# One-hot tables laid out in groups of four, and the rank phase of a graph kernel written out, on one core

## The reference

```python
edge_index = jnp.stack([src, dst])                       # dst is sorted, src is not
# layer 0: B = exp(-edge_weight); out = segment_sum(B[:, None] * x[dst], src); x = layernorm(x + out)
# layer 1: segment_sum, segment_max and mean of edge_attr_32 by src; an MLP of them; x = layernorm(x + h)
# layer 2: two graph convolutions, segment_sum by dst with degree norms; x = layernorm(x + out)
# layer 3: attention over the edges of each dst, softmax, segment_sum by dst; x = layernorm(x + y)
```

## Time and profile before

| | us |
|---|---|
| median of 3 runs (10755.75 to 10773.13) | 10757.1 |
| the profiled execution's own time | 10722.97 |
| its span | 10721.2 |
| busy: PE 27%, DVE 48%, ACT 7%, POOL 65% of the span | |
| granted clock of TensorE, mean (as a share of 2.4 GHz) | 0.547 |

### The profile page before, as it was taken

How to read it: one execution, slowest core, us unless ns; L and a number is a source line. 1 busy time by engine, 2 the same in 40 slices (tenths; PEclk the granted TensorE clock), 3 DMA queues, 4 the chain that set the end, 5 groups by cost and what they waited for, 6 DMA issues and landing times.

```text
span 10721.2 us, 73942 instructions
## 1 busy us (share of the span) xinstructions
PE 2920.0 (27%) x14214; PEld 2646.6 (25%) x14214; DVE 5184.4 (48%) x18978; ACT 768.3 (7%) x2419; POOL 6928.5 (65%) x6880
## 2 busy tenths in 40 slices
PE   9999888888600130000000200000002000000000
PEld 9998777777500130000000200000002000000000
DVE  5558777777699632222222222222224455555555
ACT  0003222222200010000000000000000000000000
POOL 0407777777700427777777577777777777777775
PEclk9995555555555565555555555555555555555555
DMA  5002222222277402222222122222221222222221
GB/s 226 12 7 77 72 72 75 72 72 75 75 272 273 144 24 54 52 52 54 52 52 54 37 53 53 52 54 52 52 54 27 60 58 61 58 61 59 59 60 37
DMA packets 541044, 766.54 MB, mean 71 GB/s; under 512 B 328408, under 2 KB 341632, under 8 KB 527600
## 3 DMA queue, kind: packets, MB, share of 16 engines
q1 hardware_dynamic: 321008, 509.44, 14.1%
q0 software_dynamic: 219904, 255.88, 11.1%
HBM read 352.03 MB, written 412.82 MB: 71 GB/s over the span
## 4 chain that ended last, share of the span: by engine, by line
POOL 62%; issue 21%; PE 9%; DVE 7%; DMA 1%; POOLq 0%; ACT 0%; DVEq 0%; SPq 0%; ACTq 0%
POOL arena_a L573 43%; POOL by_src L522 15%; PE bank L693 7%; POOL arena_a L542 3%; DVE arena_a L1096 2%; DVE arena_a L1091 2%; POOL adst_at_start L556 1%; PE bank L787 1%; PE bank L809 1%; DVE arena_b L1175 0%; DVE stat L1172 0%; DVE stat L1176 0%; DVE x L1174 0%; DVE x L1182 0%; DVE cap_blk L1053 0%
## 5 line engine op out<-in xcount | busy, mean ns | idle before, releaser
L573 POOL DMA_INDIRECT arena_a<-table_c,decay x3136 | 2968.3, 947 | 1190.5 <-issue 955.0
L1282 DVE SCALAR_TENSOR_TENSOR arena_a<-arena_a,same_dst 128x64 f32<-128x64 f32 x3134 | 893.4, 285 | 3000.3 <-DMA arena_a<-table_c,decay 2894.9
L522 POOL DMA_INDIRECT by_src<-arena_b,idx_blk x1568 | 1627.1, 1038 | 756.3 <-issue 497.4
L573 POOL DMA_INDIRECT arena_a<-table_at,decay x1568 | 1637.0, 1044 | 477.9 <-issue 477.9
L767 PE MATMUL bank<-ident,chunk_end 128*64 128x128 f32 (+2 forms) x8 | 2.7, 442 | 6147.6 <-DVEq L842 6147.6
L767 PEld LDWEIGHTS bank<-ident,chunk_end 128*64 128x64 f32 (+2 forms) x8 | 1.4, 240 | 6148.2 <-DVEq L842 6148.2
L735 PE MATMUL bank<-arena_b 98*128 98x128 f32 x3136 | 988.2, 418 | 226.0 <-DVE arena_b L992 226.0
L735 PEld LDWEIGHTS bank<-arena_b 98*128 98x128 f32 x3136 | 815.8, 310 | 277.6 <-DVE arena_b L992 277.6
L728 PE MATMUL bank<-arena_b 128*98 128x128 bf16 x1568 | 801.3, 511 | 1.6 <-ACT arena_b L654 1.0
L693 PE MATMUL bank<-arena_b 128*98 128x128 bf16 x3136 | 737.6, 415 | 16.5 <-DVE arena_b L921 16.5
L693 PEld LDWEIGHTS bank<-arena_b 128*98 128x98 bf16 x3136 | 736.8, 259 | 17.0 <-DVE arena_b L921 17.0
(11 more groups left out here) (260 smaller groups left out, 5317.7 us busy)
## 6 DMA issues: line engine op xcount, KB each, us to landing
states_src<-arena_a SPq DMA_DIRECT2D x98, 1024.0 KB, 4.8
states_c<-arena_a SPq DMA_DIRECT2D x196, 512.0 KB, 2.7
hrows<-by_src SPq DMA_DIRECT2D x98, 776.0 KB, 6.1
states_at<-arena_a SPq DMA_DIRECT2D x98, 576.0 KB, 3.3
x_at_start<-arena_a SPq DMA_DIRECT2D x7, 7168.0 KB, 48.4
arena_b<-x_at_start SPq DMA_DIRECT2D x98, 512.0 KB
arena_a<-table_c,decay POOLq DMA_INDIRECT x3136, 2.4
arena_b<-in_a SPq DMA_DIRECT2D x98, 256.0 KB, 3.5
```

The source lines that it names most:

```text
L522: pool.indirect_dma_start(out=by_src, out_offset=AT(ap=idx_blk[h][:, k:k + 1], axis=0), in_=rows[h][:, k, :], in_offset=None)\
L573: pool.indirect_dma_start(out=gb[r][:, k * w:(k + 1) * w], out_offset=None, in_=table[g], in_offset=AT(ap=src_i[:, n * J + k:n * J + k + 1 ...
L1282: ins = v.scalar_tensor_tensor(out=st[h][:, k * D:(k + 1) * D], in0=old, scalar=same_dst[:, e:e + 1], in1=gb[r][:, k * D:(k + 1) * D], op0 ...
```

## The change

- **Layout.** The one-hot tables become `[group][node digit][4 tiles]`. A matmul now reads every 4th value: its operands step by 8 bytes in place of 32. The tables of numbers are 4 wide and are repeated over the groups by the access pattern. This holds for both histograms and for the rank phase.
- **The rank phase is written out** on SP, POOL, ACT, PE and DVE, with constants for all waits. The histograms stay loops.
- **No copies.** Digits, masks and source numbers are read in place from `digits`, `same_dst` and `src_f`.
- **Four buffers** of `rows` and `idx_blk`, with `scattered0` to `scattered3`. To make room, `xs` and `xb` move from `arena_b` to `arena_a`.
- SP issues the attributes of a block one block earlier than before, right behind that block's features.

```diff
-        iota_hi = early["ih"].bitcast(bf16).rearrange("p (n t) -> p n t", t=J)
-        iota_lo = early["il"].bitcast(bf16).rearrange("p (n t) -> p n t", t=J)
+        iota_hi = early["ih"].bitcast(bf16).rearrange("p (n t) -> p n t", t=Q)
+        iota_lo = early["il"].bitcast(bf16).rearrange("p (n t) -> p n t", t=Q)
+        def in_groups(table):
+            return table.rearrange("p (g n) t -> p g n t", g=1).to_broadcast([P, J // Q, table.shape[1], Q])
+        def spread(digit, n):
+            return digit.rearrange("p (g o t) -> p g o t", o=1, t=Q).to_broadcast([P, J // Q, n, Q])
+        def one(onehot, k):
+            return onehot[:, k // Q, :, k % Q]
...
+            for n in range(-1, NBLK):
+                if n + 1 < NBLK:
+                    if n >= 1:
+                        sp.wait_ge(s("rows_ready"), n)
+                    m, h = n + 1, (n + 1) % 2
+                    sp.dma_start(early[f"xs{h}"], rows_of(x_at_start, D)[:, m * (J * D):(m + 1) * (J * D)])\
+                      .then_inc(s(f"xs_in{h}"), 16)
+                    if m >= R:
+                        sp.wait_ge(*scattered(m))
+                    sp.dma_start(rows[m % R][:, :, D:D + E32], a32_v[:, m * J:(m + 1) * J, :])\
+                      .then_inc(s(f"a32_in{m % R}"), 16)
...
-                        v.tensor_tensor(oh_hi[h], iota_hi, bf(digits[o, "hi"][:, at], HIGH), ALU.is_equal)
-                        v.tensor_tensor(oh_lo[h], iota_lo, bf(digits[o, "lo"][:, at], LOW), ALU.is_equal)\
+                        v.tensor_tensor(oh_hi[h], in_groups(iota_hi), spread(digits[o, "hi"][:, at], HIGH), ALU.is_equal)
+                        v.tensor_tensor(oh_lo[h], in_groups(iota_lo), spread(digits[o, "lo"][:, at], LOW), ALU.is_equal)\
                             .then_inc(s("onehots"), 1)
...
-                            last = pe.matmul(hist, oh_hi[h][:, :, k], oh_lo[h][:, :, k], start=False, stop=False)
+                            last = pe.matmul(hist, one(oh_hi[h], k), one(oh_lo[h], k), start=False, stop=False)
...
+            for n in range(NBLK):
+                v.wait_ge(s(f"xs_in{n % 2}"), (n // 2 + 1) * 16)
+                for quad in range(J // Q):
+                    g = n * (J // Q) + quad
+                    stage_a(g)
+                    if g:
+                        stage_b(g - 1)
+                    if quad == 1 and n + 1 < NBLK:
+                        v.wait_ge(s("hist_added"), n * J + 1)
+                        onehots_of(n + 1)
+            stage_b(L // Q - 1)
```

More of the change, by code:

```diff
@@ L320, in rows_of, with scattered @@
             return dram_ap.rearrange("(p l) w -> p (l w)", p=P)
[L322 to L324 removed]
+        def scattered(n):
+            return s(f"scattered{n % R}"), n // R * (16 * J)
         def blk(i, h):
@@ L752, in _ @@
-            pe.wait_ge(s("tile_onehots"), 1)
-            for k in range(Q):
-                turn(0, k)
-            turns(pe, body)
+            pe.wait_ge(s("tile_onehots"), 1)
+            for t in range(Q):
+                turn(t)
+            for t in range(L):
+                h, k, g = t // J % 2, t % J, t // Q
+                pe.wait_ge(s("snap_ready"), t + 1)
+                pe.matmul(hist, one(oh_hi[h], k), one(oh_lo[h], k), start=False, stop=True,
+                          skip_group_check=True).then_inc(s("hist_added"), 1)
+                if t % Q == 0:
+                    pe.wait_ge(s("hi_t_ready"), g + 1)
+                    if g >= 2:
+                        pe.wait_ge(s("selected"), (g - 1) * Q)
+                at = slice(t % Q * P, (t % Q + 1) * P)
+                last = pe.matmul(p_cnt[g % 2][:, at], hi_t[g % 2][:, at], snap[t % 2], start=True, stop=True)
+                if t % Q == Q - 1:
+                    last.then_inc(s("counted"), 1)
+                ahead = (g + 1) * Q
+                if t % Q < 2 and ahead < L:
+                    if t % Q == 0:
+                        if ahead % J == 0:
+                            pe.wait_ge(s("tile_onehots"), ahead // J + 1)
+                        if g:
+                            pe.wait_ge(s("ranked"), g)
+                    turn(ahead + t % Q * 2)
+                    turn(ahead + t % Q * 2 + 1)
@@ new lines, in stage_a @@
+            def stage_a(g):
+                for t in range(g * Q, (g + 1) * Q):
+                    n, k = t // J, t % J
+                    h = n % 2
+                    old = xb[h][:, k - 1, :] if k else xb[1 - h][:, J - 1, :] if n else first_row[:, :]
+                    if t:
+                        v.wait_ge(s("v_tiles"), t)
+                    v.scalar_tensor_tensor(out=xb[h][:, k, :], in0=old, scalar=same_dst[:, t:t + 1],
+                                           in1=xs[h][:, k, :], op0=ALU.mult, op1=ALU.add).then_inc(s("v_tiles"), 1)
+                    if t % Q == 0:
+                        v.wait_ge(s("src_spread"), g + 1)
+                    rank = v.scalar_tensor_tensor(out=junk[t % 2], in0=p_src[g % 2][:, t % Q * P:(t % Q + 1) * P],
+                                                  scalar=src_f[:, t:t + 1], in1=before[:, :],
```

218 lines of the change are left out of this document (63 added, 155 removed).

## The result

| us | before | after |
|---|---|---|
| median | 10757.61 (10755.75 to 10773.13, 4 runs) | 10349.16 (10336.82 to 10352.99, 4 runs) |
| ratio | | 0.9615, 95% interval 0.9599 to 0.9632 |
| the profiled execution's own time | 10722.97 | 10336.82 |
| its span | 10721.2 | 10335.0 |

A forecast was written before the change was run, and what follows sets the result against it. PE was taken to bound the histograms and POOL's scatters the rank phase; later passes' gathers stay untouched. Terms -310 - 4 + 0 = -314 took the median from 10757 to 10443 us, range 10370 to 10550.

The forecast's parts named there:

- the rank phase: Scatter phase limited by POOL: removed work worth nothing there, shifted meetings with DVE's instructions taken as 0, bounds -50 and +60.
- The histograms: Both histograms: smaller operand step cuts a block from 3.76 to 2.18 us, saving 310 us.
- the round's other part: Histograms' round through two buffers: 2.64 us besides PE's 16 tiles, for two blocks.
- the half clock: Histogram matmuls: 0.107 us a tile at a step of 8 bytes, taking PE at 1.2 GHz.
- The rival of a partial gain: Histograms: each new line still costs, 0.13 to 0.2 us a tile; at 0.17 saves 214, 10543 us; 14%.
- no gain: Histograms: the step doesn't matter at 8 bytes, histograms as before, 10753 us; 7%.
- slower one-hots: Grouped one-hots fall to one value a cycle on DVE: histograms +27, rank phase +162, 10942 us; 9%.
- The node scatter: POOL's 98 scatters beside the second histogram: about one a block, 214 us, ending with it; costed at nothing, no margin.
- Ahead of the first scatter: Before the rank phase's first scatter: fewer copies and less DVE waiting for PE, -4 us.
- My sign of error for this phase: Rank phase: scatters with a mean off 1038 ns by over 40 would show the prediction wrong.
- POOL's gaps at 0.30: Rank phase: POOL limited by its own 1568 x (0.959 + 0.30) us, with no waits to remove.
- The profiled execution and the median: Whole kernel: the median taken 34 us above the profiled execution, so 10409 became 10443 us.

The follow-up runs named there:

- doubled kernels: POOL scatters each tile twice, the second time into a tensor nothing reads, in the changed kernel (12311.0 us), it with features early (12348.0) and the kernel before (12667.4).
- e7_act_rows: The changed kernel with the multiplication of a block's rows by decay moved from DVE to ACT: 12152.8 us against 11792.7 for the changed kernel, with stalls.

## What the prediction had right, and where it failed

The direction and the main term were right; the time, 10349, lies 21 us below the range. The step that failed is the rank phase, put at 0 with bounds of -50 and +60: its scatters took 69.6 us less.

- **The histograms: right.** -305.3 against -310. The price of a tile was not 0.107 but 0.118, and the round's other part 2.53 us in place of 2.64 (DVE restarts earlier), so the two errors nearly cancelled: 2.21 us a block against 2.18. The reason given for 0.107, the half clock, was wrong: the granted clock was 0.78, and at 1.00 a tile takes 0.118 as well. Lines set it. With the price of a line read off 0.235/128 = 1.84 ns and 64 lines at a step of 8, the rows of before would have given 0.118, though no row of before shows that the price goes by lines. The rival of a partial gain is true in its mechanism, each new line costs, but at the price of 0.118 and not 0.17. The two rivals of no gain and of slower one-hots are false: 0.97 and 1.22 us as before.
- **The node scatter: the answer right, the mechanism too dear.** I had one scatter a block and no margin. It is 1.77 us from one to the next and 46 us of margin, since 38 of the 98 scatters aren't held up at all.
- **Ahead of the first scatter**: -5.4 against -4.
- **The rank phase: this step failed.** "At a random phase L1003 would cost about half its length, 0.6, and the pair of one-hots as much, 1.2 in all. I take 0." The multiplication did cost 0.61 where it met a scatter, 0.5 a block. (Before, it met one in 78 of 98 blocks, so it was 0.75 a block and not the 0.96 that I had.) The one-hots did not cost as much: 0.18 a block, all other meetings together 28 us, so the excess fell by 50 us, to the very bound of -50. What I had wrong is that the one-hots fall at random. They follow the multiplication at a fixed distance, and a scatter that it holds up restarts POOL at a fixed time after it (it ends 0.83 us after, the next ones follow 1.26 apart); so wherever the multiplication itself stands, the one-hots stand at the same place of a scatter. In the three kernels without stalls that have the new layout and no copies they cost 18.0, 18.4 and 18.7 us; in the kernel before, at a distance 1.00 us longer, 43.6, and doubled 27.8. With stalls POOL starts from another point, and the same one-hots cost 80. This is read from the timelines; no run changes the distance alone. That the multiplication's part is the phase, and that the phase comes from the order of two issues on SP, is shown by the doubled kernels, where it is worth 34 us; for the change itself, at 16 scatters a block, it is inferred from the same drop, 0.94 to 0.61. My sign of error for this phase, a mean off 1038 ns by over 40, was too wide: it was off by 32, which is 50 us.
- **The pauses were missed.** The longest "issue" of POOL was 2.1 us in the earlier trace rows, where all others are 0.3. I priced POOL's gaps at 0.30 throughout, and 13 pauses of 1.5 us over it were not a term of the sum. They were worth 20 us. Without POOL's loop they stay, and so they do with the new layout alone. With two buffers in the changed kernel their places come back in three runs, but at 0.32 us and not 1.5; with four buffers and one wait more a block there are 18; doubled scatters have none. So neither the number of buffers nor the loop explains them, and the increment of `pool_begun` that the change dropped was not tested. What the pause is, and which part of the change removed it, stays open.
- **The profiled execution and the median.** The profiled run of before lay 34 us below the median and I carried that over; the one of after lies 12 below. That is 22 us of the miss that no stage holds.

Together: 69.6 in the rank phase, less 5 in the histograms, 7 in the rest and 22 in the carry-over make the 94 us between 10443 and 10349. Without the pauses or without the carry-over the time would have stood at the edge of the range.

## What to carry to other kernels

Count the 16-byte lines that a TensorE operand touches, 1.84 ns each here, and lay out a table so that neighbouring columns share one; stop when the engine that writes the table is the limit. Where GpSimd's indirect DMAs set the pace, look at what releases VectorE's long two-input instructions: released by a DMA's landing they meet the next DMA at full length, and an issue moved on another queue changes that. A long instruction that follows it at a fixed distance also falls at a fixed place, so its cost is read off the timeline and not taken as an average. And read the longest wait in a row as well as the mean: thirteen pauses of 1.5 us were in plain sight.

## What was not expected of the hardware

- The step also sets VectorE's price: the pick of each edge's count, which reads PSUM and one stepped bf16 operand, took 374 ns (L992) at a step of 32 bytes and 285 at 8 (L972). With stalls it took 373 at a step of 16 and 288 at 4:

```profile
L972 DVE SCALAR_TENSOR_TENSOR arena_b<-bank,arena_b 128x128 bf16<-128x128 f32 x1568 | 390.1, 285 | 14.9 <-PE bank L733 1.4
```

- POOL pauses 1.5 us at every 112th scatter in the kernel before, 0.3 us at the same places in the changed kernel with two buffers, 1.2 us at every 80th in `e7_act_rows`, and never in the doubled kernels. The cause wasn't found.
- The kernel before took 10697 or some 12616 us on the chip numbered 7 in two sets. With stalls the changed kernel has waits of up to 11 us on ACT and DVE, and its gathers in two of the later passes take 1047 ns each in place of 946. The cause wasn't found.
